# Attention on float32r: projections of stages 2 and 3, two-part queries and keys in stages 1 and 2, and new step orders

## The reference

```
x = x + attn(norm(x))            # causal self attention, inputs and weights fake-quantized to 8 bits
x = x + xattn(norm(x), ctx)      # 120 context rows a sequence, mask, softmax with one extra zero logit
h = layer_norm(norm(x), ln1_g, ln1_b)
z = norm(x) + self_attention(h)  # float32, not causal: q = (h @ wq + bq) / 4, k, v alike
x = x + z + moe(layer_norm(z))   # 8 experts, two for each token, capacity 4096 rows
```

## Time and profile before

| | us |
|---|---|
| median of 3 runs | 5287.16 |
| profiled execution | 5298.91 |
| its span | 5297.2 |
| PE busy | 4926.9 |
| DVE busy | 3899.7 |
| ACT busy | 3865.1 |
| POOL busy | 2027.2 |

### The profile page before, as it was taken

How to read it: one execution, slowest core, us unless ns; L and a number is a source line. 1 busy time by engine, 2 the same in 40 slices (tenths; PEclk the granted TensorE clock), 3 DMA queues, 4 the chain that set the end, 5 groups by cost and what they waited for, 6 DMA issues and landing times. The chain is left out here.

```text
span 5297.2 us, 147856 instructions
## 1 busy us (share of the span) xinstructions
PE 4926.9 (93%) x45659; PEld 4001.1 (76%) x45660; DVE 3899.7 (74%) x9253; ACT 3865.1 (73%) x8215; POOL 2027.2 (38%) x1692
## 2 busy tenths in 40 slices
PE   0999999979999999889999999995799999999998
PEld 0777777758888888667777777773599999899997
DVE  7888888868888888689999999997744444344433
ACT  5899999958888888767777777773655555555554
POOL 1222232313333333234444444442144544444443
PEclk9999999989999999999999999997799999999999
DMA  6777777746666666467777777772432332323222
GB/s 189 184 188 187 190 186 189 187 125 194 196 196 197 196 197 197 138 170 185 186 185 186 183 185 186 185 185 70 52 64 47 63 57 45 64 49 64 47 47 28
DMA packets 631700, 750.63 MB, mean 142 GB/s; under 512 B 143365, under 2 KB 560334, under 8 KB 631472
## 3 DMA queue, kind: packets, MB, share of 16 engines
q1 hardware_dynamic: 575136, 679.62, 49.0%
q0 software_dynamic: 49152, 63.09, 7.3%
q10 hardware_dynamic: 7184, 5.00, 0.3%
HBM read 476.49 MB, written 272.24 MB: 141 GB/s over the span
## 5 line engine op out<-in xcount | busy, mean ns | idle before, releaser
L1762 POOL DMA_INDIRECT out_dram<-exp_gated,exp_token x256 | 419.7, 1639 | 717.6 <-ACT exp_gated L1666 377.1
L1011 DVE TENSOR_REDUCE F_tops<-F_score 128x2 f32<-128x512 f32 x1024 | 668.8, 686 | 22.6 <-PE F_score L706 14.3
L1712 DVE TENSOR_TENSOR exp_hT_lo<-exp_whole,exp_hT_hi 128x512 fp32r<-128x512 f32 x512 | 355.4, 694 | 437.1 <-ACT exp_hT_hi L1655 437.1
L871 ACT ACTIVATE F_probs<-F_scoreT 128x512 f32<-128x512 f32 x1024 | 571.4, 591 | 74.7 <-PE F_scoreT L677 73.4
L1011 DVE TENSOR_REDUCE A_tops<-A_score 128x3 f32<-128x384 f32 x1024 | 526.9, 553 | 83.9 <-PE A_score L696 65.5
L1615 PE MATMUL exp_res<-exp_w_hi,exp_hT_hi 128*128 128x256 f32 x2048 | 573.5, 280 | 0.0
L1617 PE MATMUL exp_res<-exp_w_lo,exp_hT_hi 128*128 128x256 f32 x2048 | 568.0, 277 | 0.0
L1618 PE MATMUL exp_res<-exp_w_hi,exp_hT_lo 128*128 128x256 f32 x2048 | 567.9, 277 | 0.0
L1666 ACT ACTIVATE exp_gated<-exp_y,exp_gate 128x256 f32<-128x256 f32 x256 | 109.4, 498 | 624.1 <-DVE exp_y L1736 594.5
L871 ACT ACTIVATE A_probs<-A_scoreT 128x384 f32<-128x384 f32 x1024 | 463.3, 481 | 17.2 <-PE A_scoreT L665 8.8
L1602 PE MATMUL exp_hid<-exp_xT_hi,exp_w_lo 128*128 128x512 f32 x1024 | 405.9, 396 | 0.0
(11 more groups left out here) (355 smaller groups left out, 14326.1 us busy)
## 6 DMA issues: line engine op xcount, KB each, us to landing
QS<-d_q SPq DMA_DIRECT2D x384, 192.0 KB, 3.7
KS<-d_k SPq DMA_DIRECT2D x256, 192.0 KB, 4.0
QS<-d_q SPq DMA_DIRECT2D x384, 128.0 KB, 3.8
KS<-d_k SPq DMA_DIRECT2D x256, 128.0 KB, 4.0
d_q<-A_q_parts SPq DMA_DIRECT2D x64, 384.0 KB, 3.0
d_k<-A_k_parts SPq DMA_DIRECT2D x64, 384.0 KB, 2.8
QS<-d_q SPq DMA_DIRECT2D x384, 64.0 KB, 3.6
d_q<-X_q_parts SPq DMA_DIRECT2D x64, 384.0 KB, 2.6
```

Of the source, the lines that this page charges most:

```text
L871: nc.scalar.activation(probs[m][0:KR, at:at + HB, :].rearrange("p u x -> p (u x)"), scoreT[i % TB][0:KR, 0:HB * TCOL], ACT.Exp)\
L1011: nc.vector.tensor_reduce(dst, src, AX.X, ALU.max).then_inc(score_read, 1)
L1712: v.tensor_tensor(hT_lo[:, f, :], whole[f % OB][:, :], hT_hi[:, f, :], ALU.subtract).then_inc(h_split, 1)
L1762: nc.gpsimd.indirect_dma_start(out, bass.IndirectOffsetOnAxis(token[j % (2 * XB)][:, s:s + 1], 0), gated[par][:, s, :], None, bounds_check ...
```

## The change

1. *Projections.* In X q and proj, in F q, k, v and proj are made of three float32r matmuls instead of one float32 one (`product`): high by high, high by low, low by high. The high half of an operand is a float32r copy by ACT, the low one the difference by DVE (xT, aT) or, for weights, by DVE or POOL before the first step. X's k and v stay float32. In F ln1_g is multiplied into the weights and ln1_b goes into the biases, once before the steps; ACT's xT is then one copy of 512 columns.
2. *Queries and keys* of A and X are two float32r halves in place of three bf16 parts. `STACKS[2]` puts three pairs into 48 partitions; partitions 48 to 95 are zeroed once (`fill`, from SP in iteration FIRST + 1), the contraction is still over 96 or 98 rows. In A ACT writes q_f and the high half, POOL the low one. In X ACT writes the high half straight from PSUM and DVE the low one; q_f, k_f and POOL's part are gone. F keeps its three parts. The DRAM copies have 8 bytes for each value instead of 6, the stacked tiles 48 rows of 4 bytes instead of 96 of 2.
3. *X's scores* are 122 keys wide instead of 121; the extra column is masked.
4. *Orders* of steps are new in all three stages; the rests lose their shift in A and X. mload waits for one more seed.
5. Constants of A and X are released before F.

```diff
-STACK = ((0, 3, 0), (3, 2, 1), (5, 1, 2))
+PARTS = {"A": 2, "X": 2, "F": 3}
+STACKS = {3: ((0, 3, 0), (3, 2, 1), (5, 1, 2)), 2: ((0, 2, 0), (2, 1, 1))}
...
     "X": {
-        "DVE": ("topB v mcopy maxima tok0 tok1 norm maxima maxima maxima maxima topA wo stats maxima var c0 c1 "
-              "proj c2 c3 c4 c5 maxima c6 c7 c8 maxima c9 c10 apply"),
-        "POOL": ("k_rest q_rest fetch q refetch k"),
...
+        "DVE": ("topB v maxima tok0 tok1 maxima xT0 maxima norm aT xT1 mcopy maxima wo q topA stats var maxima k "
+              "c0 c1 c2 c3 maxima c4 maxima proj c5 c6 c7 c8 c9 c10 maxima apply"),
+        "POOL": ("fetch refetch"),
...
     "F": {
-        "DVE": ("topB maxima v maxima maxima tok0 tok1 maxima maxima maxima maxima maxima topA stats var maxima "
-              "maxima proj ustats uvar maxima c0 c1 maxima c2 c3 c4 maxima c5 route c6 c7 maxima c8 c9 maxima "
-              "c10 maxima apply uapply"),
...
+        "DVE": ("topB v maxima maxima tok0 maxima maxima tok1 xT maxima maxima aT maxima maxima stats maxima "
+              "topA var maxima proj ustats maxima uvar maxima c0 c1 c2 c3 c4 maxima c5 c6 c7 route c8 maxima "
+              "c9 maxima c10 maxima apply uapply"),
...
-SHIFTED = {"A": {"k_store": 2, "q_rest": 2, "k_rest": 2},
-           "X": {"loadB": 1, "q_store": 2, "q_rest": 2, "k_store": 2, "k_rest": 2},
+SHIFTED = {"A": {"k_store": 2},
+           "X": {"loadB": 1, "q_store": 2, "k_store": 2},
            "F": {"k_store": 2, "loadB": 1, "k_rest": 2}}
...
+        QS, KS = [sb(f"QS{i}", [98, H, 256], PDT) for i in range(2)], [sb(f"KS{i}", [98, H, KP], PDT) for i in range(2)]
+        xT = [sb(f"xT{i}", [P, 2, 256], BF16 if kind == "A" else F32R) for i in range(2)]
+        q_parts, k_parts = ([sb(f"{n}_parts{i}", [P, NP, 2, w], PDT) for i in range(2)] for n, w in (("q", 256), ("k", KP)))
...
+                def fill():
+                    for t in KS:
+                        minus = C["minus" if NP == 2 else "minus_b"]
+                        sp.dma_start(plain(t[96:98, :, :]), minus[:, 0:KP].unsqueeze(1).broadcast_to([2, H, KP])).then_inc(filled, 16)
+                    if NP == 2:
+                        for t, n in [(t, 256) for t in QS] + [(t, KP) for t in KS]:
+                            sp.dma_start(plain(t[48:96, :, :]), C["zeros"][:, 0:n].unsqueeze(1).broadcast_to([48, H, n]))\
+                                .then_inc(filled, 16)
...
+                def product(out, rows, columns, start, stop):
+
+                    (a, a_lo), (b, b_lo) = rows, columns
+                    mm(out, a, b, start=start, stop=False)
+                    mm(out, a, b_lo, start=False, stop=False)
+                    return mm(out, a_lo, b, start=False, stop=stop)
...
-                                        last = mm(s[:, (2 * u + n) * KN:(2 * u + n + 1) * KN],
-                                                  q[0:96, HB * i + u, n * P:(n + 1) * P], k[0:96, HB * i + u, 0:KN],
+                                        last = mm(s[:, (2 * u + n) * KP:(2 * u + n + 1) * KP],
+                                                  q[0:96, HB * i + u, n * P:(n + 1) * P], k[0:96, HB * i + u, :],
                                                   start=False, stop=u + n == HB, skip_group_check=True)
...
+                                    if kind == "A" or (kind == "X" and name == "k"):
+                                        last = mm(W[:, m * 256:m * 256 + n], w[:, c, ms], src[:, c, 0:n],
+                                                  start=c == 0, stop=c == 1)
+                                    else:
+                                        w_rest = wq_lo if name == "q" else wk_lo
+                                        last = product(W[:, m * 256:m * 256 + n], (w[:, c, ms], w_rest[:, c, ms]),
+                                                       (src[:, c, :], xT_lo[gp][:, c, :]), c == 0, c == 1)
...
+                if kind == "F":
+                    act.wait_ge(w_scaled, 6)
+                    for i, w in enumerate(C["wF"]):
+                        nc.scalar.activation(w_hi[i][:, :, :], w[:, :, :], ACT.Copy).then_inc(w_high, 1)
...
-                            for c in range(2):
-                                last = nc.scalar.activation(xT[gp][:, c, :], W[:, c * 256:(c + 1) * 256], ACT.Identity,
-                                                            bias=C["ln1_b"][:, c:c + 1], scale=C["ln1_g"][:, c:c + 1])
+                            nc.scalar.activation(xT[gp][:, :, :], W[:, :].rearrange("p (c t) -> p c t", c=2), ACT.Copy)\
+                                .then_inc(x_cast, 1)
+                            continue
+                        elif name in ("q", "k") and kind == "X":
+                            parts, cast, out, n = (q_parts, q_cast0, q_out, 256) if name == "q" else (k_parts, k_cast0, k_out, KT)
+                            need(act, out, 16 * (g - 1))
+                            nc.scalar.activation(parts[gp][:, 0, :, 0:n], W[:, :].rearrange("p (m t) -> p m t", m=2)[:, :, 0:n],
+                                                 ACT.Copy, scale=0.25 if name == "q" else 1.0).then_inc(cast, 1)
...
                         elif name == "xT":
                             drained(g - 2, "v")
-                            for c in range(2):
-                                last = nc.scalar.activation(xT[gp][:, c, :], W[:, c * 256:(c + 1) * 256], ACT.Identity,
-                                                            bias=C["ln1_b"][:, c:c + 1], scale=C["ln1_g"][:, c:c + 1])
+                            nc.scalar.activation(xT[gp][:, :, :], W[:, :].rearrange("p (c t) -> p c t", c=2), ACT.Copy)\
+                                .then_inc(x_cast, 1)
+                            continue
+                        elif name in ("q", "k") and kind == "X":
+                            parts, cast, out, n = (q_parts, q_cast0, q_out, 256) if name == "q" else (k_parts, k_cast0, k_out, KT)
+                            need(act, out, 16 * (g - 1))
+                            nc.scalar.activation(parts[gp][:, 0, :, 0:n], W[:, :].rearrange("p (m t) -> p m t", m=2)[:, :, 0:n],
+                                                 ACT.Copy, scale=0.25 if name == "q" else 1.0).then_inc(cast, 1)
+                            continue
                         elif name in ("q", "k"):
...
+                if kind == "F":
+                    pool.wait_ge(bias_ready, 4)
+                    for i in range(3):
+                        for c in range(2):
+                            nc.gpsimd.tensor_scalar(C["wF"][i][:, c, :], C["wF"][i][:, c, :], C["ln1_g"][:, c:c + 1], None, ALU.mult)\
+                                .then_inc(w_scaled, 1)
+                    for i in range(4):
+                        pool.wait_ge(w_high, i + 1)
+                        nc.gpsimd.tensor_tensor(w_lo[i][:, :, :], C["wF"][i][:, :, :], w_hi[i][:, :, :], ALU.subtract)\
...
+                            if NP == 2:
+                                split = q_split if name == "q" else k_split
+                                nc.gpsimd.tensor_tensor(parts[gp][:, 1, :, 0:n], src[:, :, 0:n], parts[gp][:, 0, :, 0:n], ALU.subtract)\
+                                    .then_inc(split, 1)
+                                pool.wait_ge(split, g + 1)
+                                continue
...
```

More of the change, by code:

```diff
@@ L320 @@
-        "DVE": ("topB maxima v maxima maxima maxima maxima maxima maxima tok0 maxima maxima topA tok1 maxima "
+        "SP": ("rowsB k_store fetch tok1 loadA rowsA loadB q_store"),
+        "PE": ("v pv1 xT attend maxima attend maxima maxima attend attend rowsB attend maxima maxima attend q "
+              "maxima attend maxima maxima attend tok0 tok1 maxima attend k maxima attend attend maxima pv0 "
+              "maxima attend rowsA maxima attend maxima attend maxima attend maxima attend"),
@@ L321 @@
+        "ACT": ("evac1 attend attend seed attend attend xT rowsB attend seed attend q attend seed attend attend "
+              "attend attend k seed attend rowsA attend seed attend evac0 attend attend"),
+        "DVE": ("topB maxima v maxima maxima maxima maxima maxima maxima maxima tok0 maxima tok1 maxima topA "
               "maxima maxima maxima norm maxima maxima maxima"),
-        "POOL": ("k_rest q_rest k q"),
+        "POOL": ("k q"),
     },
     "X": {
-        "SP": ("fetch loadB k_store rowsB q_store mload refetch ctxT loadA stats rowsA proj"),
@@ L332 @@
-        "POOL": ("k_rest q_rest fetch q refetch k"),
+        "SP": ("fetch loadB mload refetch rowsB k_store q_store ctxT loadA rowsA stats proj"),
+        "PE": ("v pv1 attend maxima rowsB maxima tok0 tok1 xT0 attend maxima ctxT maxima aT attend xT1 attend "
+              "yT q wo maxima attend attend k maxima maxima proj rowsA attend maxima pv0 attend"),
+        "ACT": ("seed seed evac1 seed rowsB seed xT0 attend attend ctxT aT xT1 attend seed yT attend seed q "
+              "attend seed k seed attend rowsA attend evac0 attend"),
@@ L340 @@
```

(4 more changed lines are left out.)

251 lines of the change are left out of this document (163 added, 88 removed).

## The result

The changed kernel takes 5601.3 us (median, 5595.7 to 5605.8; four runs) against 5287.3 for the kernel before (four runs; 5287.16 was of three): a ratio of 1.0593, 95% interval 1.0574 to 1.0611. The forecast was slower, 5446, range 5260 to 5540. The direction held, the size didn't: 314 us instead of 159.

What follows compares the result with a forecast made beforehand. PE was taken to bound A and X, DVE to bound F. A +58, X +67, F +19 and once +15 make +159 us: 5458 from the profiled 5298.9, 5446 against the runs' median; range 5260 to 5540.

Steps and rivals of the forecast that it cites:

- A float32r load of 128 columns holds the engine at 0.112: A's attend and X's maxima and attend: least distance after narrow matmuls; adds 1.85 us a step in A, 1.8 in X.
- ACT, DVE and POOL are below 14, so PE stands alone and idles less than now, 0.65: A: PE stream 15.65 plus 0.65 idle makes a step of 16.3 us, +0.9 a step, +58 us.
- DMA: issued two steps ahead, hidden: Query and key loads cost nothing; if that cover were gone, 0.26 MB at 188 GB/s is 1.4 us a step.
- Work tiles are now released by DVE; this is in the idle share: Several units: PE's next-but-one unit waits for DVE's order instead of ACT's; no separate price, counted within idle time.
- F: +19 forecast: F: DVE holds the step at 21.6 us, 19.5 plus stalls and waiting; +0.3 a step, +19 us.
- The wait of 0.5 us behind ACT's xT write: F: DVE's new xT half behind tok1 waits for transposes and ACT's cast, some 0.5 us a step.
- Rival 4: F alone follows PE, 19.8 us a step: stalls vanish, -96 us instead of +19; total 5331; chance 0.11.
- Once: Setup: operand tile fills, 6 us each in A and X, F's weight preparation 3; together 15, between 0 and 35.
- Rivals 2 and 3: Narrow float32r matmuls in A and X: load stays hidden, 5289, chance 0.12; or they run like float32, 5863, chance 0.09.
- Rival 1: All stages: new orders close PE's gaps, steps of 15.65, 16.7, 19.8 us; -39 us, 5248; chance 0.10.
- rival 5: F held by DVE with all stalls, 22.7 us: +90 instead of +19, 5517; chance 0.58 together with the forecast.
- The forecast's own upper end for F, 22.7: F's upper bound a step: DVE with all stalls 22.2 us and 0.5 of waiting; lower bound 19.8, PE alone.

Runs made afterwards that it cites:

- e1: A kernel of nothing but matmul streams of varied types and columns; float32r with 128 weight columns 0.112 us apart, with 64 or 32 columns 0.060.
- e5: Changed kernel with the 256-column key matmul of A's attend issued before the 128-column one: 5595 us, ratio 1.059.
- e6: Changed kernel with e5's swap, A's two 128-column causal matmuls merged into one of 256, X's four mask matmuls into two: 5566 us, ratio 1.053.
- e16: Changed kernel whose score loads in A and X fetch only 32 of 48 rows, same matmuls: 5620 us, ratio 1.063.
- e17: As e16, fewer bytes, with the merged causal and mask matmuls of e6: 5531 us, ratio 1.046.
- e14: As e12, A as before, with zeros for the low halves of X's product operands, no DVE step, ACT releasing the work tile: 5267 us, ratio 0.995.
- e12: X in its old order with three bf16 parts and float32r products; A as before but causal matmuls merged; F changed: 5622 us, ratio 1.063.
- e13: Changed kernel with the two halves of queries and keys in A and X stored as bf16, orders untouched: 5373 us, ratio 1.015.
- e9: Changed kernel's orders in A and X with three bf16 parts and float32 projections as before; F changed: 5450 us, ratio 1.030.
- e7: A as before; X with three bf16 parts, float32r products and DVE low halves in the new order; F changed: 5359 us, ratio 1.014.
- e15: As e12 without A's merged matmul, with norm behind the low halves of xT0 and aT in X's DVE order: 5529 us, ratio 1.045.

## Why the forecast missed

- **"A float32r load of 128 columns holds the engine at 0.112": right** (e1: 0.112; 64 columns 0.060). So was the list of places. The term was sized a little low: the 256-column distance is 0.120, not the 0.113 of the earlier trace rows, and the mixed stream of A's attend takes 0.41 against my 0.39. By starts A's stream grew by about 0.13 x 16 + 0.03 x 11 (the maxima without ACT's seed, 0.28 to 0.30) = 2.4 us a step, not 1.85. In X the four maxima grew by 0.23 on average, not 0.17: with the attend 1.8 + 0.5 = 2.3 us, not 1.8, and the products gave 0.5, not 0.74: 1.8 against my 1.06.
- **The step that failed: "ACT, DVE and POOL are below 14, so PE stands alone and idles less than now, 0.65".** It took 0.95 us a step off A's price and is the larger part of A's miss: A's step went from 15.4 to 17.5, so of 2.4 us of stream only 0.3 was taken in by idle time. That is 0.65 of the 1.2 us a step by which A missed; the other 0.55 is the stream's size. Under-used engines didn't close PE's gaps here; I read the gaps as handovers in a written order. e5 and e6 show it from the other side: 0.8 and 1.7 us a step off PE's stream came back as 0.1 and 0.4. X's step went up by 2.4 against 1.8 of stream: its idle time, which I had left almost as it was, grew by 0.5. Over both stages the idle terms and the sizes of the stream have about equal shares of the miss.
- **"DMA: issued two steps ahead, hidden": wrong in A as soon as PE gets shorter.** e16 and e17 put 22 and 55 us on the bytes. I had the price, 0.26 MB at the rate of the window for 1.4 us a step, and no row for what stands behind a load in the same queue: the top rows' DMA.
- **"Work tiles are now released by DVE; this is in the idle share": no price where one was due.** With the low halves themselves, and with the lower clock that came with the waits, it is the difference between 1021 (e14) and 1377 (e12) of X in the old order. In the new order, which was laid out around it, PE waits 0.5 us for X_tok and 0.3 for X_aT_lo a step; e13 leaves 51 us of X's loss with order, low halves and releases.
- **F: +19 forecast, -17 measured.** The low halves cost 1.2 us of DVE as said and never stretched (0.69 and 0.68 us each, in every step), the stalls fell from 2.65 to 1.7 (1.28, 0.51 and 0.43 beside 0.17), topB kept its 1.1. The wait of 0.5 us behind ACT's xT write, which I had put in, didn't come: DVE reads xT at once. Rival 4's 19.8 didn't come either.
- **Once: +35, not +15.** The zeros for A's key tiles take 6 us of SP's queue and its next load as long:

```profile
107.60 6.18 SPq L564 DMA_DIRECT2D A_KS<-zeros  x2
113.83 6.27 SPq L599 DMA_DIRECT2D A_xin<-in_x_dram  x1
```
- Rivals 2 and 3 are excluded by the distances (0.112; neither 0.056 nor 0.22). Rival 1 is excluded by A, whose step lies 1.3 us above its stream (13.8 + 2.4), rival 5 by F's 20.9. The forecast's own upper end for F, 22.7, was the only place where the range went up; A and X had none, though both of their idle terms were chosen, not read.

Open: what lengthens X's wait with fewer bytes; which handovers make the 88 us of e9 in A; how much of X's last 51 us is the order and how much the low halves.

## What to carry to other kernels

A 32-bit stationary operand of 128 columns needs some 0.11 us for its load, so it wants a matmul of 256 columns in front; count distances in the very sequence, not type by type. Do not credit a busy engine with the idle time it had before when the work of others shrinks: in this kernel with its written order most of it stayed. Look at the granted clock before you put a longer step down to its waits. When an engine becomes the reader that frees a shared tile, price everything in front of it in its queue, and when bytes grow, ask which small transfer stands behind the large ones.

## What the runs showed of the hardware

- Alternating types cost extra: pairs of bf16 and float32r with 128 columns repeat every 0.187 us, against 0.056 + 0.112 alone; with 256 columns 0.244 against 0.229.
- A float32r product of 256 columns runs 0.120 apart, 0.109 in bf16.
- Where PE waited long in a step, the granted clock fell. It was 1.00 in X before, after, in e7, e9, e13 and e14; in X of e12, where PE waits 2.5 us in one place of each step, it was 0.85, so some of it ran at 1.2 GHz and the rest at 2.4. In e15 a step at 0.92 took 20.9 us beside 19.6 at 1.00. For e12 the cost is only estimated, as above, since none of its steps ran at full clock:

```profile
1300.00:2200.00 900.00, 757.89 (x7132) 631.67 (x7130) 618.32 (x1619) 596.61 (x1336) 250.44 (x244) 0.85 0.52 146
```
